# Graph-network kernel: where the edge counts are turned and how the second layer's gather banks are cut

## The reference

```python
# block 0: two relational layers, norm from counts of (type, dst)
for l in range(2):
    W = jnp.einsum('rb,bdf->rdf', w_coe[l], bases[l])
    T = jnp.einsum('nd,rdf->rnf', h, W)
    agg = jax.ops.segment_sum(T[etype, src] * norm, dst, num_segments=N)
    h = relu(batchnorm(agg + h @ self_loop[l]))
x = layernorm(x + h)
# block 1: x + segment_sum(x[dst], src)
# block 2: attention over edges; softmax per dst needs the greatest score among a node's edges
# block 3: segment_sum(x[src] + edge_attr, dst)
```

## Time and profile before

| | us |
|---|---|
| median of three runs | 5907.89 (5897.45 to 5912.18) |
| the profiled execution, its own time | 5911.12 |
| its span | 5909.4 |
| first layer, about | 228 to 2745 |
| second layer, about | 2785 to 4103 |

### The profile page before, as it was taken

How to read it: one execution, slowest core, us unless ns; L and a number is a source line. 1 busy time by engine, 2 the same in 40 slices (tenths; PEclk the granted TensorE clock), 3 DMA queues, 4 the chain that set the end, 5 groups by cost and what they waited for, 6 DMA issues and landing times. The chain is left out here.

```text
span 5909.4 us, 157242 instructions
## 1 busy us (share of the span) xinstructions
PE 4289.3 (73%) x54120; PEld 3252.4 (55%) x54121; DVE 4190.3 (71%) x9549; ACT 1869.0 (32%) x2646; POOL 2482.1 (42%) x2045
## 2 busy tenths in 40 slices
PE   5666667666666666664999999997983666666697
PEld 2345445544445445443666666665442666666687
DVE  4377777777777777776777777776116999999823
ACT  2111111111111111111666666664001555555500
POOL 0477666666666666661000000000000777777400
PEclk9788788787787788786999999998996888888899
DMA  5444444444444444444777777775963344444388
GB/s 199 163 136 129 128 129 123 120 127 127 128 130 127 128 129 119 125 127 128 244 243 246 246 244 246 243 247 183 303 218 111 120 152 152 152 152 152 117 282 253
DMA packets 701393, 1008.83 MB, mean 171 GB/s; under 512 B 147635, under 2 KB 607774, under 8 KB 688126
## 3 DMA queue, kind: packets, MB, share of 16 engines
q1 hardware_dynamic: 618290, 779.49, 41.3%
q0 software_dynamic: 56448, 115.72, 7.8%
q10 hardware_dynamic: 26572, 112.71, 4.9%
HBM read 728.15 MB, written 279.47 MB: 171 GB/s over the span
## 5 line engine op out<-in xcount | busy, mean ns | idle before, releaser
L619 POOL DMA_INDIRECT f_rows<-table,f_recs x1715 | 1685.4, 983 | 924.2 <-issue 623.6
L710 PE MATMUL f_acc<-f_rows,f_hot 128*128 128x264 f32 x3430 | 1133.3, 492 | 739.4 <-DVE f_rows L946 710.3
L710 PEld LDWEIGHTS f_acc<-f_rows,f_hot 128*128 128x128 f32 x3430 | 812.1, 246 | 949.1 <-issue 479.3
L2004 PE MATMUL a_psum<-state_and_spare,a_weights 128*128 (+1 forms) x4802 | 654.5, 306 | 304.6 <-DVE a_weights L2122 164.4
L1954 POOL TENSOR_TENSOR a_weights<-a_powers,a_counts 128x896 f32<-128x896 f16 x245 | 718.1, 2936 | 343.8 <-ACT a_powers L2044 317.5
L2004 PEld LDWEIGHTS a_psum<-state_and_spare,a_weights 128*128 128x128 f32 x4802 | 644.1, 222 | 318.0 <-issue 215.4
L1194 ACT ACTIVATE g_grow<-g_gps 128x1024 f16<-128x1024 f32 (+1 forms) x637 | 629.8, 989 | 442.6 <-PE g_gps L1126 442.6
L1142 PE MATMUL g_zps<-g_ohot,g_grow 32*128 32x256 f16 x19992 | 661.3, 269 | 14.5 <-ACT g_grow L1194 14.5
L1109 POOL DMA_INDIRECT g_grow<-high_low_rows,g_lcur x49 | 61.1, 1246 | 1330.0 <-PE g_zps L1142 1215.7
L1142 PEld LDWEIGHTS g_zps<-g_ohot,g_grow 32*128 32x128 f16 x19992 | 459.7, 93 | 176.5 <-issue 124.4
L1238 DVE TENSOR_SCALAR g_ohot<-count,slot_target 128x256 f16<-128x256 f16 x2499 | 530.7, 281 | 0.2 <-PE g_zps L1142 0.2
(11 more groups left out here) (273 smaller groups left out, 5921.8 us busy)
## 6 DMA issues: line engine op xcount, KB each, us to landing
f_rows<-in_edge_attr SPq DMA_DIRECT2D x343, 320.0 KB, 3.2
g_srow<-slot_sources SPq DMA_DIRECT2D x245, 320.0 KB, 4.8
counts_by_source_f<-state_and_spare ACTq DMA_DIRECT2D x49, 1568.0 KB, 7.1
state_and_spare<-counts_by_source_f SPq DMA_DIRECT2D x343, 224.0 KB, 3.7
counts_by_destination_f<-state_and_spare SPq DMA_DIRECT2D x343, 224.0 KB, 2.4
no_edge_penalty<-g_pen SPq DMA_DIRECT2D x343, 224.0 KB, 2.7
s_ring<-counts_by_destination_f SPq DMA_DIRECT2D x98, 784.0 KB, 4.3
a_pen<-no_edge_penalty SPq DMA_DIRECT2D x49, 1568.0 KB, 10.1
```

Of the source, the lines that this page charges most:

```text
L619: e.indirect_dma_start(out=rows[:, j, 0:D], out_offset=None, in_=k.table_d[0], in_offset=bass.IndirectOffsetOnAxis(ap=recs[:, j, 4:5].bitc ...
L710: m = e.matmul(acc[:, 0:GW], hot[:, j, :], rows[:, j, :], start=j == 0, stop=j == SLOTS - 1)
L2004: m = e.matmul(psum[:, 4 + i // 3, i % 3 * (D + 4):i % 3 * (D + 4) + D + 1], weights[:, j, i * P:(i + 1) * P], k.msg[:, bass.ds(hb * SEG + ...
```

## The change

It does four things.

1. **First layer, turning.** After `count`, a new `turn_counts` on TensorE turns pieces of `mine` into a PSUM bank of its own, `flipped`: one piece of seven transposes at the end of every group. Pieces 0 to 3 of tile t - 1 come in groups 3 to 6 (`FLIP_AT`), pieces 4 to 6 of tile t - 2 in groups 0 to 2 (`FLIP_LATER`). ScalarE's new `move_turned` copies each piece to `by_dst`, makes the penalty from the same bank with a Relu, and issues two stores. `mine` is stored in four DMAs, one a block.
2. **First layer, the row of numbers.** The new bank takes the place of `count_up`'s: `count_up` and `eighths` are now views of `k.count16` in SBUF. `earlier` shares the memory of `put_row`.
3. **Second layer.** Everything that turned counts is gone: SP's loads and stores, `turn_counts`, the copies and penalties. The gather uses three banks of two cells (`PAIRS`, 25 a tile); ScalarE copies a pair at a time.
4. **Penalties** change sign and size (`FAR` from -3.0e38 to -1.0e34), and `sweep` subtracts with its operands swapped.

```diff
-FAR = -3.0e38
+FAR = -1.0e34
...
-        earlier = sb("earlier_hits", [P, QUADS, NT], F16)
         put_row = sb("put_row", [P, QUADS, 3, QW], F16)
+        earlier = put_row[:, :, :, :].rearrange("p a x r -> p (a x r)")[:, 0:QUADS * NT].rearrange("p (a j) -> p a j", j=NT)
...
-        count_up = cells(pb("count_up", [P, 512])[:, :], False)
-        eighths = count_up.rearrange("p (j e) -> p j e", e=RELATIONS)[:, :, 0]
+        count_up = k.count16[:, 0:P]
+        eighths = k.count16[:, :].rearrange("p (j e) -> p j e", e=RELATIONS)[:, :, 0]
+        flipped = pb("flipped", [P, 512])[:, :].bitcast(F16)[:, 0:SW]
...
+        FLIP_AT = {3: 0, 4: 1, 5: 2, 6: 3}
+        FLIP_LATER = {0: 4, 1: 5, 2: 6}
...
+            def turn_counts(t, g):
+                e.wait_ge(cnt_moved, t * (len(BLOCKS) * QUARTERS) + blocks_of(g) * QUARTERS)
+                e.wait_ge(by_dst_moved, t * NSEG + g)
+                for i in range(SEG):
+                    m = e.transpose(flipped[:, i * P:(i + 1) * P], mine[:, g * SEG + i, :], k.ident16[:, :])
+                m.then_inc(turned, 1)
...
                         if 2 <= g < 2 + len(BLOCKS):
                             count(t - 1, g - 2)
+                        if g in FLIP_AT:
+                            turn_counts(t - 1, FLIP_AT[g])
+                        elif not second:
+                            turn_counts(t - 2, FLIP_LATER[g])
...
+            def move_turned(t, g):
+                w = g % FLIP_SLOTS
+                e.wait_ge(turned, t * NSEG + (g + 1))
+                e.wait_ge(by_dst_out[w], (t * slot_uses(g) + g // FLIP_SLOTS) * 32)
+                e.activation(by_dst[:, w, :], flipped, ACT.Copy)
+                e.activation(pen[:, w, :], flipped, ACT.Relu, bias=far[:, 0:1], scale=FAR)
+                e.drain().then_inc(by_dst_moved, 1)
+                e.wait_ge(by_dst_moved, t * NSEG + (g + 1))
+                for to, row in ((k.cd_d[False], by_dst), (k.pen_d, pen)):
+                    e.dma_start(to[bass.ds(t, 1), :, g * SW:(g + 1) * SW].rearrange("a p c -> (a p) c"), row[:, w, :])\
+                     .then_inc(by_dst_out[w], 16)
...
+                if not first:
+                    move_turned(t - 1, 6)
+                e.wait_ge(stored, t * (len(BLOCKS) * 16))
                 for b, (lo, n) in enumerate(BLOCKS):
                     e.wait_ge(counted, t * len(BLOCKS) + (b + 3))
...
+                    e.wait_ge(cnt_moved, t * (len(BLOCKS) * QUARTERS) + (b + 1) * QUARTERS)
+                    e.dma_start(k.cs_d[False][bass.ds(t, 1), :, lo * P:(lo + n) * P].rearrange("a p c -> (a p) c"),
+                                mine[:, lo:lo + n, :].rearrange("p j d -> p (j d)")).then_inc(stored, 16)
+                    if b:
+                        move_turned(t, b - 1)
+                move_turned(t, len(BLOCKS) - 1)
...
-        gps = pb("gps", [P, 2, 512])
-        tps = pb("tps", [P, 512])[:, :].bitcast(F16)[:, 0:SW]
+        GBANKS = 3
+        gps = pb("gps", [P, GBANKS, 512])
...
+        PAIRS = [(c, min(c + 2, LEFT)) for c in range(0, LEFT, 2)]
...
-                def gather(t, b):
-                    e.wait_ge(g_sb, t * NB + b)
...
+                def gather(t, h):
+                    lo, hi = PAIRS[h]
+                    e.wait_ge(s_made, t * SPIECES + ((hi - 1) // SPIECE + 1))
+                    e.wait_ge(g_sb, t * NPAIR + (h + 1 - GBANKS if h >= GBANKS else 0))
...
+                        for h in pairs(b):
+                            gather(t, h)
+                        for h in pairs(b - 1):
+                            scatter(t, h)
...
+                        for h in pairs(b):
+                            e.wait_ge(g_ps, t * NPAIR + (h + 1))
+                            e.activation(grow[:, gslot(b), PAIRS[h][0] % BATCH:(PAIRS[h][1] - 1) % BATCH + 1, :],
+                                         gps[:, h % GBANKS, :].rearrange("p (i f) -> p i f", i=2), ACT.Copy).then_inc(g_sb, 1)
...
-                e.tensor_tensor_reduce(out=pen[:, w, :], in0=pen[:, w, :], in1=frow,
-                                       scale=1.0, scalar=FAR, op0=ALU.add, op1=ALU.max, accum_out=best[:, i:i + 1])
+                e.tensor_tensor_reduce(out=pen[:, w, :], in0=frow, in1=pen[:, w, :],
+                                       scale=1.0, scalar=FAR, op0=ALU.subtract, op1=ALU.max, accum_out=best[:, i:i + 1])
```

More of the change, by code:

```diff
@@ L574, in phase_first @@
         cnt = pb("cnt", [P, QUARTERS, 512])
+        FLIP_AT = {3: 0, 4: 1, 5: 2, 6: 3}
+        FLIP_LATER = {0: 4, 1: 5, 2: 6}
+        blocks_of = lambda g: next(b + 1 for b, (lo, n) in enumerate(BLOCKS) if (g + 1) * SEG <= lo + n)
+        slot_uses = lambda g: len(range(g % FLIP_SLOTS, NSEG, FLIP_SLOTS))
         rec_in = [sem(f"rec_in{g}") for g in range(GROUPS)]
@@ L625, in _ @@
         def _(e):
-            for i in range(4):
-                m = e.transpose(count_up[:, i * P:(i + 1) * P], k.column16[:, i, :], k.ident16[:, :])
-            m.then_inc(ring, GROUPS)
+            e.sem_inc(ring, GROUPS)
             e.sem_inc(counted, 2)
@@ L700, in self_terms, with tile @@
                 e.matmul(pm[:, P:2 * P], ht[:, :], k.loop[:, 1, :], start=True, stop=True).then_inc(t_ps, 1)
-            def tile(t, first):
+            def tile(t, first, second):
                 for g in range(GROUPS):
@@ L749, in _, with tile @@
             e.wait_ge(self_out, 16)
-            e.wait_ge(blank, 1)
-            with e.Fori(0, NT) as t:
+            e.wait_ge(blank, 2)
+            def move_turned(t, g):
[9 more added lines that the diff above has]
+                     .then_inc(by_dst_out[w], 16)
+            def tile(t, first):
                 e.wait_ge(placed, t + 1)
@@ L763, in _ @@
                              bias=k.minus1[:, 0:1]).then_inc(key_out, 1)
+                if not first:
+                    move_turned(t - 1, 4)
                 e.wait_ge(ht_ps, t + 1)
                 e.activation(ht[:, :], pm[:, 0:P], ACT.Copy).then_inc(ht_sb, 1)
+                if not first:
+                    move_turned(t - 1, 5)
                 e.wait_ge(t_ps, t + 1)
@@ L769, in _ @@
                 e.dma_start(k.attr_d[:, bass.ds(t * P, P)], agg[:, D:2 * D]).then_inc(attr_out, 16)
-                e.wait_ge(stored, t * 16)
+                if not first:
+                    move_turned(t - 1, 6)
+                e.wait_ge(stored, t * (len(BLOCKS) * 16))
                 for b, (lo, n) in enumerate(BLOCKS):
@@ L1027, in phase_second @@
         srow_in = [sem(f"srow_in{i}") for i in range(SPIECES)]
-        cs_in = [sem(f"cs_in{g}") for g in range(NSEG)]
-        stored = [sem(f"stored{g}") for g in range(NSEG)]
         s_made, g_ps, g_sb, o_made, scattered = sem("s_made"), sem("g_ps"), sem("g_sb"), sem("o_made"), sem("scattered")
@@ L1078, in run @@
                 e.dma_start(k.hl_d.rearrange("(t p) f -> p t f", p=P), hl[:, :, :]).then_inc(hl_out, 16)
-                for g in range(NSEG):
-                    counts(0, g)
-                def tile(t, final):
-                    for g in range(NSEG):
-                        if not final and g < SPIECES:
-                            e.wait_ge(s_made, t * SPIECES + (g + 1))
-                            piece(t + 1, g)
-                        if not final:
-                            e.wait_ge(turned, t * NSEG + (g + 1))
-                            counts(t + 1, g)
-                        store(t, g)
                 with e.Fori(0, NT - 1) as t:
-                    tile(t, False)
-                tile(NT - 1, True)
-                for g in range(NSEG):
-                    e.wait_ge(stored[g], NT * 32)
+                    for i in range(SPIECES):
+                        e.wait_ge(s_made, t * SPIECES + (i + 1))
+                        piece(t + 1, i)
                 e.wait_ge(hl_out, 16)
```

135 lines of the change are left out of this document (49 added, 86 removed).

## The result

The changed kernel takes 6019.56 us (median of four runs, 6016.88 to 6019.73) against 5910.03 us before: a ratio of 1.0188, 95% interval 1.0170 to 1.0205. It is 1.9% slower. I had forecast 5868 us, faster, with a range of 5765 to 6010 us: the result lies 10 us above the range, close to what rival 2 gave.

A forecast was written before the change was run, and what follows sets the result against it. GpSimd, needing 55.1 us a tile, was to bound the first layer, and TensorE the second. 5911 + 187 (first layer) - 231 (second) + 4 (between) = 5871, less 3 for the median: 5868 us, range 5765 to 6010.

The forecast's parts named there:

- rival 2: First layer: gathers lock in phase with long VectorE instructions, holds of 14 us in place of 11.3, 5998 us; chance 25%.
- hold of the gathers: First layer, GpSimd: gathers delayed by VectorE instructions with two SBUF inputs, 11.3 us a tile, 1.3 of it already today.
- TensorE-VectorE loop with the turning: First layer: from 51.2 to about 53.2 us a tile, as block 0 waits on ScalarE for the last turned piece.
- second-layer tile: Second layer, paced by TensorE: from 26.6 to 21.9 us without turns and with three banks, -231 us over 49 tiles.
- where the layers meet: Between the layers: +12 us for pieces turned after the last tile, -8 for a wait that goes, together +4.
- Their own time should not change: First layer: VectorE instructions reading count_up and eighths keep their length when these move from PSUM to SBUF.
- longer VectorE durations: Sign named in advance: the prediction is wrong if the listed VectorE instruction durations grow in the profile after.
- the prediction's own rule: First layer: mean hold of gathers is d - 0.12 - 0.63 us for a VectorE instruction of duration d over 1.37.
- the sum breaks even: The first layer's loss and the second's gain cancel at a gather hold of 12.2 us a tile, against 11.3 expected.
- Rival 1: First layer: gathers are not held, the loop of 53.2 us sets the pace, +96 in place of +187, 5777 us; 20%.
- Rival 3: First layer: gathers hold VectorE up too, 5.6 us more in the loop, 58.8 a tile, 6046 us; chance 8%.
- The turning: First layer, TensorE and ScalarE: costs nothing while GpSimd is later, 96 us if the GpSimd cost were absent.

The follow-up runs named there:

- before_eighths_in_sbuf: The kernel before, with eighths alone read from SBUF at the step of eight and count_up left in PSUM: 6084.74 us, 1.0294 of before.
- number 2: The kernel before, with count_up and eighths as views of the SBUF row, step of eight kept, nothing turned in the first layer: 6227.76 us, 1.0529.
- dense_halves: The changed kernel with eighths as a dense SBUF row and the large VectorE instructions with two SBUF inputs cut in two: 5848.09 us, 0.9882 of before.
- number 7: First layer of the kernel before with the second layer of the changed one, turning left out, counts read by source: 5663.83 us, 0.9576 of before.
- number 8: The kernel before with loads, turns, moves and stores of the counts taken out of the second layer, its two banks kept: 5786.10 us, 0.9779.

## Why the prediction was wrong, point by point

| step | predicted | measured |
|---|---|---|
| length of the instructions that read eighths | 2.29 and 2.20 us | 3.83 and 3.62 |
| hold of the gathers, a tile | 11.3 us | 14.1 |
| first-layer tile | 55.1 us, +187 | 58.05, +329 |
| TensorE-VectorE loop with the turning | 53.2 us | 54.5, with 0.4 of halves |
| second-layer tile | 21.9 us, -231 | 21.9, -231 (49 tiles of 4.72) |
| where the layers meet, and behind the second | +4 | +14 and -6 |

**The step that failed** is "Their own time should not change". I drew it from one pair, L856 in PSUM and L858 in SBUF, both of which read neighbouring values, and let it stand for L842 and L805, which read every eighth value. The trace of before has no large instruction that reads SBUF with such a step, so this was an operation without a row of its own, and it should have been bounded from both sides like the others. It does have small ones, which I overlooked: L801 reads 40 fp32 values of the records, 20 bytes apart, and L822 is of the same kind without a step.

```profile
L801 DVE SCALAR_TENSOR_TENSOR f_jk<-f_wrec,f_inw x49: 221/222/225, 216.9 to 2674.5; 128x40 f32<-128x40 f32 x49
...
L822 DVE SCALAR_TENSOR_TENSOR f_second<-f_rank,f_own x49: 191/193/224, 253.1 to 2710.3; 128x40 f32<-128x40 f32 x49
```

The 29 ns between them are 0.73 ns a value, and 2040 values of that would make 1.5 us, the 1.54 that L842 grew by. It was a hint and no price: a tensor_scalar of 40 values takes 184 ns with this step (L793) and without (L821). The prediction did name the sign, longer VectorE durations, as one of those by which it would be wrong.

The rest of the chain to the bound is sound: by the prediction's own rule, with d = 3.83 and 3.62 the mean holds are 3.08 and 2.87 us in place of 1.54 and 1.46, and 11.3 + 3.0 = 14.3, where 14.1 were measured. 43.8 + 14.3 = 58.1 us a tile gives 5908 + (58.1 - 51.2) x 48 - 231 + 4 = 6012 us, and 6016 with the 14 and -6 of the last row in place of 4; the runs gave 6020. One slip of little weight: the sum breaks even at a hold of 12.1 us, not 12.2.

- **The hold of the gathers, and GpSimd as the bound: right.** That gathers would be held, and by how much for a given length, came out in nine kernels within 0.8 us a tile: 11.3 by the rule and 10.7, 10.7, 10.5 and 11.7 measured with a dense or free step, 14.3 and 14.1, 13.8, 14.1 and 13.6 with a costly one, 7.3 and 7.3 in before_eighths_in_sbuf. Rival 1 (no hold) is out. The Trainium skill's inference that tensor_tensor doesn't hold up descriptors (SBUF — State Buffer, Who interferes with whom) doesn't fit these gathers.
- **Rival 2** gave 5998 us and its hold of 14 us, nearly the result, but not its mechanism: with eighths dense the hold is 10.7 and 11.7 us on either side of the mean rule. Had I bet on it, I would have come near the number for a wrong reason.
- **Rival 3: wrong.** The large instructions that got a second SBUF input and read neighbouring values kept their length, at gathers without a pause: L987 with 2048 elements takes 2.28 us before and after, L976 (L916 before) 1.79, and L918 still 1491 to 1493 ns.
- **The turning: free while GpSimd is the bound**, as said (0.4 us a tile by number 2). Bare, its loop takes 3.3 us a tile more than before in dense_halves, 0.4 of it for the halves, so 2.9 where I had 2.0. The place was right, ahead of block 0, and so was the wait of TensorE there (1.75 us, 1.8 predicted); what I left out is that VectorE also waits 1.0 us a tile longer for ranks (6.3 in place of 5.3). With block 0 first nearly all of it goes: 51.6 us a tile.
- **The second layer: right in each term**, and shown apart by numbers 7 and 8. For the added semaphore waits, which had no row, 12.5 x 0.55, 12.75 x 0.98, 1.9 and 0.58 leave 0.1 us of the 21.9, where I took 0.2.
- **Where the layers meet:** from L858 to L1203 it was 102.3 us, in number 7 90.0. Of the 12.3 us less, 4.7 are the first tile of the second layer, which lies between the two marks, so the eight us at the second layer's start did go (7.6). The pieces that are turned behind the last tile took 21.7 us (111.7 - 90.0) in place of 12, as each takes ScalarE some 3.0 us and TensorE waits for it. That makes +14, or +9 between the marks. Behind the last L1209 the time is 6 us shorter, which I had not forecast; in number 8 it is 7 us shorter too (1802.9 us behind the last L1185, 1809.9 before), so it goes with the turning that the second layer no longer has at its end.

## What to carry to other kernels

When an operand moves from PSUM to SBUF, look at two things that its shape doesn't show: whether the instruction now has two SBUF inputs while GpSimd issues indirect gathers (each gather that started under it waited until 0.12 us before its end), and the step in bytes between the values it reads (in this instruction 8 was free and 16 cost two thirds more). An engine with slack is a bound in waiting: compare each engine's need per tile with the pace, and if two needs come out near one another, mend both, since either alone shows nothing. A second copy of 51 values, dense, turned a change that lost 1.9% into one that won 0.9%, and with the long instructions in halves and block 0 first it won 3.7%.

## What the runs showed of the hardware that I had not expected

- The tensor_tensor that compares a row of fp16 values in SBUF with a column takes 1.12 ns an element when the row is dense or has a step of 8 bytes, and 1.88 to 1.89 ns with a step of 16 or 32 bytes (2040 elements: 2.29, 2.29, 3.83, 3.85 us). With the row in PSUM the step of 16 bytes took 2.29 us.
- A gather gets through between two VectorE instructions that follow at once: one that met the first half was 0.36 us late, with the second half close behind, and in halves the hold fell from 10.7 to 6.1 us a tile. What the 0.12 us before an instruction's end are, no run here shows.
